# Layers 1 and 3 of a four-layer kernel: TensorE's block between two value products goes from score, maxima, score, maxima to maxima, score, score, maxima

## The reference

```
xn = layernorm(x);  s = attn(xn);  g = silu(ffn(xn));  x = x + s * g
```

```
scores = einsum('bqhd,bkhd->bhqk', q, k) * scale      # layer 1
out = einsum('bhqk,bkhd->bqhd', softmax(scores), v);  out @ Wo.T
```

## Time and profile before

| what | us |
|---|---|
| median of 3 runs (lowest, highest) | 5156.76 (5155.24, 5166.38) |
| profiled execution, its span | 5170.1, 5168.8 |
| PE busy | 4542.4 (88%) |
| DVE busy | 3147.9 (61%) |
| ACT busy | 2499.2 (48%) |
| POOL busy | 2318.8 (45%) |

### The profile page before, as it was taken

The page is one execution under the profiler, slowest core; times in us unless marked ns, Lnnn a source line. Parts: engine busy times, 40 slices in busy tenths (PEclk is TensorE's granted clock), DMA queues, the critical chain, the costliest instruction groups (busy, mean ns, idle before and its releaser), DMA issues. The chain is left out here.

```text
span 5168.8 us, 68806 instructions
## 1 busy us (share of the span) xinstructions
PE 4542.4 (88%) x27376; PEld 2215.6 (43%) x27376; DVE 3147.9 (61%) x4176; ACT 2499.2 (48%) x3813; POOL 2318.8 (45%) x1323
## 2 busy tenths in 40 slices
PE   5999999977886777858799999978799999999997
PEld 3444444445654333323322222224455555555554
DVE  4656565636765777752477777843465665565663
ACT  2344444436663555642266666652244444445443
POOL 0455555558771577870100000000066666666675
PEclk8999999989997999979799999988799999999998
DMA  1000000011110000000000000000000000000000
GB/s 32 3 3 3 3 3 3 3 29 32 37 28 12 2 2 2 1 5 19 3 2 2 1 2 1 1 9 1 10 3 3 3 1 3 3 3 1 3 1 9
DMA packets 61954, 36.81 MB, mean 7 GB/s; under 512 B 36308, under 2 KB 53888, under 8 KB 61376
## 3 DMA queue, kind: packets, MB, share of 16 engines
q1 hardware_dynamic: 61632, 32.41, 2.5%
HBM read 22.03 MB, written 1.05 MB: 4 GB/s over the span
## 5 line engine op out<-in xcount | busy, mean ns | idle before, releaser
L795 DVE TENSOR_REDUCE L_part<-banks 128x2 f32<-128x1024 f32 (+2 forms) x1600 | 1881.5, 1189 | 965.7 <-PE banks L646 825.0
L780 ACT ACTIVATE L_weights<-banks 128x1024 f32<-128x1024 f32 (+1 forms) x1600 | 1581.1, 1001 | 1056.4 <-PE banks L678 816.1
L704 PE MATMUL banks<-L_weights,L_V 128*32 128x512 f32 (+3 forms) x6400 | 1490.3, 602 | 3.6 <-ACT L_raw L729 1.8
L1002 POOL TENSOR_TENSOR L_wsum<-L_wsum,L_weights 128x1024 f32<-128x1024 f32 (+1 forms) x448 | 995.0, 2221 | 55.8 <-ACT L_weights L780 3.0
L985 POOL TENSOR_TENSOR L_wsum<-L_wsum,L_two 128x1024 f32<-128x1024 f32 x240 | 571.0, 2379 | 841.6 <-DVE L_two L969 838.5
L704 PEld LDWEIGHTS banks<-L_weights,L_V 128*64 128x64 f32 (+1 forms) x6400 | 282.3, 122 | 453.5 <-issue 397.0
L678 PE MATMUL banks<-L_QH,L_KH 64*128 64x512 f32 (+3 forms) x1664 | 432.0, 453 | 17.9 <-issue 10.2
L2513 POOL MEMSET F_xr<- 128x16 f32 x1 | 0.1, 127 | 933.4 <-POOLq L97 933.4
L646 PE MATMUL banks<-L_KH,L_QH 64*128 64x512 f32 (+3 forms) x1664 | 372.5, 429 | 31.7 <-ACT L_weights L780 17.5
L678 PE MATMUL banks<-L_QL,L_KH 64*128 64x512 f32 (+3 forms) x1664 | 372.0, 382 | 0.0
L678 PE MATMUL banks<-L_QH,L_KL 64*128 64x512 f32 (+3 forms) x1664 | 371.7, 381 | 0.0
(11 more groups left out here) (446 smaller groups left out, 5911.7 us busy)
## 6 DMA issues: line engine op xcount, KB each, us to landing
F_early<-F_V SPq DMA_DIRECT2D x63, 128.0 KB, 2.3
F_tab<-xpos SPq DMA_DIRECT2D x8, 512.0 KB, 4.4
F_h<-L_ffn_h_w SPq DMA_DIRECT2D x2, 1024.0 KB, 8.0
F_wqkv<-L_ffn_wqkv SPq DMA_DIRECT2D x2, 768.0 KB
L_cos<-rope_cos SPq DMA_DIRECT2D x1, 1024.0 KB, 5.0
L_sin<-rope_sin SPq DMA_DIRECT2D x1, 1024.0 KB, 7.0
out<-X SPq DMA_DIRECT2D x1, 1024.0 KB, 5.1
F_z<-F_x SPq DMA_DIRECT2D x32, 31.8 KB
```

Of the source, the lines that this page charges most:

```text
L704: mm = pe.e.matmul(O[r, c:BANK], self.V[g % 2][:, kt, h, :], self.W[x % self.NW][:, y, c:BANK], start=kt < starts, stop=kt >= tiles - starts)
L780: act.e.activation(self.W[x % self.NW][:, :, c:BANK], self.banks(it)[:, :, c:BANK], ACT.Exp, scale=self.scale).then_inc(self.exped, 1)
L795: dve.e.tensor_reduce(self.part[n % 3][:, pr, j, p, :], self.banks(it)[:, :, 0:wide], AX.X, ALU.max).then_inc(self.mx_read, 1)
L1002: pool.e.tensor_tensor(acc[:, :, c:BANK], acc[:, :, c:BANK], W[:, :, c:BANK], ALU.add).then_inc(self.summed, 1)
```

## The change

`MIRRORED` is off by default and on in layers 1 and 3. Where it is on, the pieces at the end of a round come ahead of the score. A group is then P1 S1 S2 P2.

```
+    MIRRORED = False
...
-                items += mid + eager(ys[-1:]) + two + ps[half:]
+                items += mid + eager(ys[-1:]) + (ps[half:] + two if self.MIRRORED else two + ps[half:])
...
 class NormedAttention(WideAttention):
...
-    EAGER = True
+    EAGER = MIRRORED = True
...
 class LatentAttention(SummedAttention):
...
-    EAGER = True
+    EAGER = MIRRORED = True
```

## The result

| what | before | after |
|---|---|---|
| median, us (lowest to highest) | 5156.0 (5153.2 to 5166.4) | 5204.65 (5198.6 to 5209.3) |
| ratio after/before, 95% interval | | 1.009 [1.0076, 1.0105] |
| profiled execution, its span | 5170.1, 5168.8 | 5209.3, 5208.0 |
| layer 1, first to last exponential | 587.5 | 650.9 (+63.4) |
| layer 3, the same | 1375.3 | 1355.2 (-20.1) |

The kernel became slower by 0.9%, 48.7 us by the medians. Of the stretches outside the two layers the start became 5.6 us shorter, and the others changed by less than 2 us each.

The account below looks back on a forecast made before the run. PE was taken to bound layer 3, and the chain between engines layer 1. Layer 1's +36 and layer 3's -22 gave +14 us, 5171 us on the median of 5156.8; range 5146 to 5202.

Parts of the forecast that it names:

- first joins: Layer 3, 30 groups with a first join: 5.61 us against 5.24, so -0.37 each, -11 us.
- P2 waits for the maximum in layer 3 too: Rival: DVE late by 0.4 us or more after layer 3's pair sums, 32 us less gain, 5200 us; chance 0.05.
- Layer 1's loop: Layer 1: P1, maximum, P2, values, P1, where everything DVE has ahead of P1's maximum counts; P2 can go after 1.82 us.
- the term of layer 1: Layer 1's 128 groups together: +36 us, bounds +15 to +60.
- 30 plain groups behind a pair sum: Layer 1: the pair sum delays P1's maximum, so P2 goes at 4.10 instead of 3.29; +0.85 taken each, +25 us.
- 12 q groups: Layer 1, groups with a q for the queries: two remainders stand ahead of P1's maximum; +1.4 each, +17 us.
- 6 groups with two key products: Layer 1: DVE's remainders bound bank 7 anyway; +0.7 each, +4 us.
- 14 denominators: Layer 1, groups with denominators: transpose and reciprocal stand ahead of P1's maximum; +0.3 each, +4 us.
- 28 joins: Layer 1: divisions on ACT held back S1's exponential, and P2 with it; -0.2 each, -6 us.
- The pair sum at 1.22 us: Layer 1: a slower layer leaves POOL idle more often, pair sum nearer 1.22 than 1.75 us; +25 rather than +40 us.
- -8, POOL gets time that it lacks: Layer 1: the slower pace gives POOL time that it lacks in the longest chunks; -8 us.
- layer 1's clock: Rival: 18 q groups of layer 1 run value products at half clock, +18, 5189; with mean pair sums 5205; chance 0.13.

Follow-up runs that it names:

- e6: The changed kernel with added products of zeros behind the second score of each layer 1 group (the filled version): 5184.3 us, ratio 1.0037 to the kernel before.
- e7: The changed kernel with POOL's additions of single weights in layer 1 cut to 16 of 512 columns per head: 5138.7 us, ratio 0.9958 to the kernel before.
- e10: The kernel before, old order in both layers, with POOL's single-weight additions in layer 1 cut to 16 of 512 columns per head: 5134.3 us, ratio 0.9936.

## Why the prediction was wrong

**Right.**
- What bounds the layers, and that P2's wait passes from the exponential to the maximum.
- Layer 3: -20.1 for -22. The plain group was forecast at 4.38 and is 4.39 (median); the q group +0.45, measured +0.45; first joins -0.37 and -0.36; second joins -0.2 and -0.21. The rival in which P2 waits for the maximum in layer 3 too did not happen.
- Layer 1's loop: the first plain group behind a pair sum lasts 4.07 to 4.09 in 7 of 11 chunks and 4.09 in all 11 of e6 (4.10 forecast). The q group lasts 7.12 or 7.13 (7.1 forecast) in all 14 q groups of the changed kernel and e6 that have no time at half clock.

**Wrong: the term of layer 1**, +36 forecast and +63.4 measured. By its parts, in sums over the groups:

| part | forecast | measured |
|---|---|---|
| 30 plain groups behind a pair sum | +25 | +39.5 |
| 12 q groups | +17 | +24.9 |
| 6 groups with two key products | +4 | +9.8 |
| 14 denominators | +4 | +1.8 |
| 28 joins | -6 | -11.7 |
| all other groups (forecast: time given back by POOL) | -8 | -0.9 |

Two steps failed.
- *The pair sum at 1.22 us.* The prediction had both values, +25 at 1.22 and +40 at the mean of 1.75, and took the first with the argument that a slower layer leaves POOL idle more often. POOL is idle more often (busy for 465.55 of 663 us, 474.23 of 599 before), and the pair sum still takes 1757 ns on the mean. What counts is not how busy POOL is but whether one of its additions runs when the pair sum is issued. In the third place of a chunk they were long before too, 1909 ns on the mean, with the group behind them at 3.89 us; the new order made them 2572 and, above all, put them ahead of the maximum for which P2 waits. The section "Who interferes with whom" of the Trainium skill's page "SBUF — State Buffer", which says that the two exclude each other for the whole instruction, agrees with the trace: the pair sum ends 1.09 us after the addition that was running, and the addition behind it takes 2.24 us. It was the inference from it to an average that was wrong. e7 and e10 show its size: of the 63 us, 27 are there only with POOL's additions. The term "-8, POOL gets time that it lacks" fails with it. The wait that it counted on did shrink, from the 27.9 us of the earlier trace rows to this:

```profile
ACT L_weights L781 <- POOL L_wsum L1003: 6.5, 4, 2.3
```

But the groups outside the listed ones together are only 0.9 us shorter for it, so it had not been holding the layer back.
- *The clock, left out of the forecast.* The rival "layer 1's clock" had the mechanism and its price: +18 for the 18 q groups at half clock, 5189, and 5205 with the pair sums at their mean. The kernel takes 5204.65. That this is within 0.4 us is partly luck: the figure holds the -8 that did not come and is counted from a median, while the profiles explain 39 of the 48.7 us. I gave this rival 0.13, and my range ended at 5202, though I wrote that it reaches to the clock's figures: 5189 lies in it, 5205 does not. Measured, the two kinds of q groups cost 34.7 for the 21 forecast, and the filled version, which keeps the clock, takes 18.3 us of these back (98.1 to 86.4 and 55.1 to 48.5). The prediction's own rows spoke for it: layer 1 was at 0.94 with a wait of 1.4 us in its q group, and the change made this wait 3.2 us.

The two overlap, since a long pair sum is also a wait in which the clock falls (e7 has 101 us at half clock, the changed kernel 166): the 34 us of the estimate for the clock and the 27 for the additions must not be added up.

**Open.** The 0.33 us for each us at half clock are a line through three points with changed orders; how the 34 us lie over the groups is not shown beyond the q groups and the first and seventh places. No run has both the zero products and the short additions, so what the new order costs in layer 1 with neither effect was not measured. Why the stretch ahead of layer 3 has less half-clock time in 5 of the 16 profiled executions, with the same code, was not tried.

## What to carry to other kernels

Where an order is turned so that a product waits for another engine's result, list what stands in that engine's queue ahead of the result, place by place, and give each instruction the duration that it has when it collides, not the mean or the shortest. Here the pair sum was 1.22 us where it met no addition, and the rest of the addition plus 1.08 us where it met one. Where a stretch's granted clock is under 1.00 already, price each new wait of TensorE twice, once as a wait and once as the products behind it at the lower level. The same order can be right in a layer where TensorE is busy to 98% and wrong in one where it is busy to 79%, so switch it by layer.

## What the runs showed of the hardware

More work made the kernel faster: 936 products of zeros took 26 us off layer 1, by bringing its granted clock from 0.87 to 0.97, and the same products cost 3 us where little time was at 1.2 GHz. And a pair sum, 1.22 us by itself, took 2.92 us in the row above and up to 3.29 us elsewhere in layer 1. How long it takes is set by what is left of GpSimd's running addition: in 36 of the 37 cases of the changed kernel's layer 1 it ended 1.08 to 1.10 us after that addition, and a lower busy share of GpSimd (70% for 79%) left the mean where it was, 1757 ns for 1752.
